# Sixteen-head cross-attention: rows of the stacks split by head parity, and the largest scores sought on four quarters of the array

## What is computed

```
q = rope(norm(x) @ cq.T)   split in 16 heads of 8 features
k = rope(ctx @ ck.T), v = ctx @ cv.T
scores = einsum('bqhd,bkhd->bhqk', q, k) / sqrt(8)
scores = where(mask, -inf, scores);  w = softmax(scores)
out    = einsum('bhqk,bkhd->bqhd', w, v)
```

## Time and profile before

| | us |
|---|---|
| median of 3 runs | 6767.78 |
| lowest and highest run | 6764.62, 6768.18 |
| the profiled execution | 6758.11 |
| its span | 6756.3 |

### The profile page before, as it was taken

The page is one execution under the profiler, slowest core; times in us unless marked ns, Lnnn a source line. Parts: engine busy times, 40 slices in busy tenths (PEclk is TensorE's granted clock), DMA queues, the critical chain, the costliest instruction groups (busy, mean ns, idle before and its releaser), DMA issues.

```text
span 6756.3 us, 141162 instructions
## 1 busy us (share of the span) xinstructions
PE 6176.6 (91%) x56181; PEld 4441.0 (66%) x56181; DVE 3931.5 (58%) x8705; ACT 3318.7 (49%) x6385; POOL 2240.2 (33%) x2179
## 2 busy tenths in 40 slices
PE   5799999999999999999979899999689999989998
PEld 4466666666666656666644777777457777766983
DVE  2677777777777777777755244444434444444553
ACT  1466656666566566665643234444223333333763
POOL 3555555555555555555520000000001111137440
PEclk6799999999999999999989799999789999998998
DMA  1566656656566566665730000000000000021000
GB/s 46 89 103 95 101 96 101 101 90 109 87 102 109 86 99 102 98 102 90 116 68 18 13 33 33 28 33 24 13 25 13 15 15 10 15 76 39 2 1 22
DMA packets 396487, 407.88 MB, mean 60 GB/s; under 512 B 125575, under 2 KB 372946, under 8 KB 393786
## 3 DMA queue, kind: packets, MB, share of 16 engines
q1 hardware_dynamic: 395834, 398.85, 33.3%
HBM read 158.00 MB, written 0.46 MB: 23 GB/s over the span
## 4 chain that ended last, share of the span: by engine, by line
PE 70%; DVE 9%; POOL 7%; issue 6%; ACT 4%; DMA 2%; SPq 1%; POOLq 1%; DVEq 0%; ACTq 0%
PE psum L2205 10%; PE psum L2172 9%; PE psum L1546 6%; PE psum L1534 6%; PE psum L1520 6%; PE psum L2217 4%; PE psum L1560 4%; PE psum L1568 3%; PE psum L1666 3%; POOL slot_context L3361 2%; DVE row_max L1885 2%; PE psum L435 2%; PE psum L421 2%; PE psum L1675 1%; DMA key_stack<-key_parts 1%
## 5 line engine op out<-in xcount | busy, mean ns | idle before, releaser
L1885 DVE TENSOR_REDUCE row_max<-psum 112x1 f32<-112x500 f32 x2304 | 1443.7, 669 | 282.8 <-PE psum L1534 277.7
L2003 ACT ACTIVATE weights<-psum 125x448 f32<-125x448 f32 x2304 | 1154.0, 544 | 764.0 <-PE psum L1520 749.7
L1520 PEld LDWEIGHTS psum<-query_stack,key_stack 121*125 121x125 bf16 x9216 | 829.0, 140 | 367.6 <-issue 165.7
L1534 PE MATMUL psum<-key_stack,query_stack 97*112 97x500 bf16 x2304 | 906.9, 394 | 102.8 <-DVE row_max L1885 81.9
L1520 PE MATMUL psum<-query_stack,key_stack 121*125 121x112 bf16 x9216 | 931.3, 224 | 70.1 <-ACT weights L2003 64.9
L2729 POOL TENSOR_TENSOR l_ctx_v<-l_ctx_v,l_ctx_w 125x512 f32<-125x512 f32 x48 | 60.9, 1269 | 2292.0 <-DVE l_ctx_v L2723 2292.0
L2205 PE MATMUL psum<-l_ctx_v,l_turned 125*128 125x128 f32 x5376 | 713.8, 281 | 16.0 <-ACT l_turned L2243 12.4
L2285 DVE TENSOR_REDUCE l_stat<-psum 128x1 f32<-128x1500 f32 (+1 forms) x224 | 391.7, 1748 | 573.4 <-PE psum L2172 573.4
L2205 PEld LDWEIGHTS psum<-l_ctx_v,l_turned 125*128 125x128 f32 x5376 | 643.3, 191 | 58.7 <-ACT l_turned L2243 40.0
L1546 PE MATMUL psum<-weights,values 125*17 125x112 f32 x18432 | 677.3, 265 | 0.2 <-ACT weights L2003 0.2
L1546 PEld LDWEIGHTS psum<-weights,values 125*17 125x17 f32 x18432 | 379.2, 97 | 263.1 <-ACT weights L2003 144.8
(11 more groups left out here) (526 smaller groups left out, 10283.8 us busy)
## 6 DMA issues: line engine op xcount, KB each, us to landing
key_stack<-key_parts SPq DMA_DIRECT2D x1728, 125.0 KB, 4.4
ctx_t<-in_ctxT SPq DMA_DIRECT2D x96, 750.0 KB
l_ctx_v<-in_ctxV SPq DMA_DIRECT2D x32, 750.0 KB
query_stack<-query_parts SPq DMA_DIRECT2D x576, 28.0 KB, 3.6
l_ctx_t<-in_ctxT SPq DMA_DIRECT2D x16, 750.0 KB
slot_context<-in_ctxV SPq DMA_DIRECT2D x16, 750.0 KB
key_stack<-ctx_mask_rows SPq DMA_DIRECT2D x576, 3.9 KB
sm_w<-in_sm_w SPq DMA_DIRECT2D x3, 2048.0 KB
```

Source lines behind the costliest of these rows:

```text
L1520: mm = e.matmul(self.k.psum[0:KN, h, (p % 4) * QC:(p % 4 + 1) * QC], ks[:, p, kt * KN:(kt + 1) * KN], q[:, p * QC:(p + 1) * QC])
L1534: e.matmul(self.k.psum[0:QC, 2 + n % 2, 0:500], q[0:ROWS_MAX, p * QC:(p + 1) * QC], ks[0:ROWS_MAX, p, c * 500:(c + 1) * 500]).then_inc(sel ...
L1885: e.tensor_reduce(self.largest[:, i % PAIRS, i // PAIRS:i // PAIRS + 1], k.psum[0:QC, 2 + i % 2, 0:500], AX.X, ALU.max, negate=True).then_ ...
L2003: e.activation(half(self.p[kt % 2], h), self.k.psum[0:KN, h, 0:HALF], ACT.Exp).then_inc(self.exped.sem, 1)
```

## The change

The stack of a pair now has 128 rows: 64 for each head of the pair. In each half, the six parts' 8 rows lie at rows 0, 8, 16, 24, 48 and 56, the mask at row 32, and 12 rows of maxima (three parts of one head's maxima for each two neighbouring pairs, four times) behind it; rows up to 47 are filled with zeros. Each DMA that wrote 16 rows becomes two that write 8. The largest scores of four heads (two pairs) are found by four matmuls of 64 rows by 64 columns, on the four quarters of the array, into two banks with 128 partitions; they are issued together, once a step, after the first score group, and wait until both banks of the step before are read. The extra rows of the query stack must be clear of the last use's maxima while the maxima are sought, which two new VectorE copies do for each slot (`clear_vector`, at kt = 7).

The core of the diff:

```diff
+PAIRS, F1 = H // 2, D // H
+PART_ROW = (0, 8, 16, 24, 48, 56)
...
-            self.k_stack = [sb(f"key_stack{i}", [ROWS_ALL, PAIRS, L], BF16) for i in range(3)]
-            self.q_stack = [sb(f"query_stack{i}", [ROWS_ALL, PAIRS * QC], BF16) for i in range(3)]
+            self.k_stack = [sb(f"key_stack{i}", [128, PAIRS, L], BF16) for i in range(3)]
+            self.q_stack = [sb(f"query_stack{i}", [128, QW + 8], BF16) for i in range(3)]
...
         for i, j in enumerate(K_PARTS):
-            e.dma_start(dst[F2 * i:F2 * i + F2, :, c * 500:(c + 1) * 500], part[:, j, :]).then_inc(sem, 16)
+            for h in range(2):
+                row = 64 * h + PART_ROW[i]
+                e.dma_start(dst[row:row + F1, :, c * 500:(c + 1) * 500], part[64 * h:64 * h + 64, j, :]).then_inc(sem, 16)
...
             for n in range(6):
-                e.dma_start(dst[ROWS:ROWS + 1, :, n * 250:(n + 1) * 250],
-                            self.mask_rows[6 * b + n:6 * b + n + 1, :].unsqueeze(1).broadcast_to(
-                                [1, PAIRS, 250])).then_inc(self.mask_stacked.sem, 16)
+                for row in (32, 96):
+                    e.dma_start(dst[row:row + 1, :, n * 250:(n + 1) * 250],
+                                self.mask_rows[6 * b + n:6 * b + n + 1, :].unsqueeze(1).broadcast_to(
+                                    [1, PAIRS, 250])).then_inc(self.mask_stacked.sem, 16)
...
         for i, part in enumerate(Q_PARTS):
-            e.dma_start(dst[F2 * i:F2 * i + F2, :].rearrange("j (p c) -> j p c", p=PAIRS),
-                        self.q_part[:, part, :]).then_inc(sem, 16)
+            for h in range(2):
+                row = 64 * h + PART_ROW[i]
+                e.dma_start(dst[row:row + F1, 0:QW].rearrange("j (p c) -> j p c", p=PAIRS),
+                            self.q_part[64 * h:64 * h + 64, part, :]).then_inc(sem, 16)
...
     def max_tensor(self, e, b, n):
...
+            e.wait_ge(self.cleared.sem, self.cleared(b))
...
-        if (b, n) > (0, 1):
-            e.wait_ge(self.max_read.sem, self.max_read(b, n) - 2)
-        e.matmul(self.k.psum[0:QC, 2 + n % 2, 0:500], q[0:ROWS_MAX, p * QC:(p + 1) * QC],
-                 ks[0:ROWS_MAX, p, c * 500:(c + 1) * 500]).then_inc(self.max_scored.sem, 1)
+        if (b, n) > (0, 0):
+            e.wait_ge(self.max_read.sem, self.max_read(b, n) - 1)
+        for h in range(2):
+            for j in range(2):
+                lo = (p + j) * QC + h * S
+                mm = e.matmul(self.k.psum[64 * j:64 * j + 64, 2 + h, 0:500], q[64 * h:64 * h + 64, lo:lo + 64],
+                              ks[64 * h:64 * h + 64, p + j, c * 500:(c + 1) * 500])
+            mm.then_inc(self.max_scored.sem, 1)
...
                     if 0 <= s < NS:
                         self.score_tensor(e, s, kt, h)
-                    if self.max_at(s, kt):
-                        b, n = self.max_at(s, kt)
-                        self.max_tensor(e, b, n + h)
+                    if h == 0 and self.max_at(s, kt):
+                        self.max_tensor(e, *self.max_at(s, kt))
...
+    def clear_vector(self, e, b):
+
+        if b >= 3:
+            e.wait_ge(self.scored.sem, self.scored(b - 3, KT - 1, 1))
+        for h in range(2):
+            op = e.tensor_copy(self.others(b, h, 16), self.no_max[64 * h + 32:64 * h + 48, :].unsqueeze(2).unsqueeze(
+                3).broadcast_to([16, TWOS, 2, S]))
+        op.then_inc(self.cleared.sem, 1)
...
-        e.tensor_copy(self.q_stack[b % 3][ROWS:ROWS_ALL, :].rearrange("r (p c) -> r p c", p=PAIRS),
-                      rows.unsqueeze(1).broadcast_to([1 + 3 * PAIRS, PAIRS, QC])).then_inc(self.side.emptied(*key), 1)
+        for h in range(2):
+            op = e.tensor_copy(self.others(b, h, OTHERS_USED), rows[32 * h:32 * h + OTHERS_USED, :, :].unsqueeze(
+                1).broadcast_to([OTHERS_USED, TWOS, 2, S]))
+        op.then_inc(self.side.emptied(*key), 1)
...
-                        e.tensor_reduce(self.largest[:, i % PAIRS, i // PAIRS:i // PAIRS + 1], k.psum[0:QC, 2 + i % 2, 0:500], AX.X,
+                        e.tensor_reduce(self.largest[:, TWOS * h + p // 2, c:c + 1], k.psum[:, 2 + h, 0:500], AX.X,
                                         ALU.max, negate=True).then_inc(self.max_read.sem, 1)
                 self.fixed_vector(e, s, kt)
+                if kt == 7 and 3 <= s + 2 < NS:
+                    self.clear_vector(e, s + 2)
```

## The result

The changed kernel takes 7636.52 us, the median of 4 runs (7628.34 to 7651.61), beside 6767.98 us for the kernel before (4 runs): a ratio of 1.1286 with a 95% interval of 1.1265 to 1.1307. It is slower by 868 us. The profiled execution took 7628.34 us, its span is 7626.5 us, against 6758.11 and 6756.3 before.

The account below looks back on a forecast made before the run. SyncE's DMA issues were taken to bound the changed kernel: 96 slots of 42.7 us make 4099, less 3241 now, +858 on 6758 gives 7616, about 7625 us with the median's 9.7. The range was 7260 to 8090.

Parts of the forecast that it names:

- Does half the size halve the issue? The rows say no.: SyncE's queue: a half-size copy holds it as long as a full one, taken as 0.705 us an issue.
- 42.7 us a slot: SyncE's time for 60 issues at 0.705 us plus 0.4 for the fetch, above the 34.3 that TensorE needs.
- the key chain at kt 10 and 11: Steps feeding the next slot's first key copy, partly at low clock: nothing to 2 us a slot, taken as nothing.
- The prologue, "2 us": Longer memsets of the prologue, together with the transpose of the maxima once a slot, were costed at 2 us.
- VectorE's work: Split rows copy and two clearing copies add 0.6 to 1.9 us a slot, taken as 0.8, hidden beside TensorE.
- I take the four as one: TensorE's four quarter matmuls run side by side and take 0.22 us a step together.
- The change of shape: TensorE: each change costs 0.08 us; two more a step make 184 us over 1152 steps.
- the gain of 58 us on TensorE: Quarters gain 242 us, less 184 for changes of shape, leaving 58, not reaching the sum because of SyncE.
- rival B: SyncE: half-size issues take half the time and stay hidden, so TensorE's gain shows: 6526 to 6710 us; chance 0.06.
- Rival A: Transfers bound too: copies to 8 partitions move at 63 GB/s, 47.5 us a slot, 8087 us; chance 0.27.
- The two directions of the waits: SyncE's waits are eaten up; TensorE waits once a slot, at kt = 10, for query DMAs, idling some 8 us.

Follow-up runs that it names:

- e1_tiny: The kernel before, with a copy of three rows of 32 bytes to scratch behind each of a slot's 30 stack copies, so 60 issues: 7633.51 us.
- e6_noclear: e2_rows16 without the two clearing copies of a slot: 6988.14 us.
- e4_own: e2_rows16, but each bank's two quarter matmuls wait only for the reduction of their own bank: 6993.94 us.
- e8_full: e4_own with two matmuls over the whole array in place of the four quarters: 6885.86 us.
- e2_rows16: The changed kernel with 30 issues a slot again, each part copied by one DMA of 16 rows, only row 32 getting the mask: 7011.64 us.
- e9_order: The kernel before with both full largest-score matmuls behind the second score group: 6806.88 us.
- e5_order: e4_own with the four quarter matmuls moved behind both score groups, next to the value products: 6900.57 us.

## Why the prediction was right

The forecast was 7625 us, the measured median is 7636.5, and the mechanism is the one forecast: e1_tiny has the issues and nothing else of the change, and takes 7633.5 us. That the number is within 12 us is partly luck, as errors of opposite sign met. Point by point:

- **"Does half the size halve the issue? The rows say no."** Right: 609 ns for 62.5 KB, 649 ns for three rows of 32 bytes (e1_tiny). The shape did matter a little, 567 against 623 ns for masks of four and of eight pairs, which was not foreseen.
- **42.7 us a slot.** From the first key copy to the last are 4320.6 - 211.8 = 4108.8 us, 42.8 a slot. The number came out so near because two parts offset each other: an issue took 0.68 us with its gap ((4108.8 - 152) / 96, less 0.4, over 60), not 0.705, and SyncE still waited 1.6 us a slot, which had been taken as nothing: about 1 us before the first key copy of most slots, the key chain at kt 10 and 11, and some 5 us in most second slots of a phase, which TensorE sets.
- **The prologue, "2 us".** Mis-sized: the first key copy comes 16.9 us later. The copies of ones start 15.5 us later, behind VectorE's first six clearing copies, and hold SyncE 703 ns each, not 640. The six take 16.2 us where later ones take 0.55 each, and nearly all of it is in two: one takes 2.9 us and ends at 55.9 us, the next takes 10.3 us and ends at 66.2 us. Two of GpSimd's memsets of the key stack, 10 us each, end at 55.7 and 65.9. So VectorE seems to have stood until GpSimd was done; no run tests it. The lines view of VectorE for 40 to 75 us has the six as its costliest group:

```profile
L1810 DVE COPY query_stack<-no_max 16x448 bf16<-16x448 bf16 x6 | 16.2, 2698 | 0.2
```

- **VectorE's work.** The two rows copies take 0.38 us each and the two clearing copies 0.55: 1.25 us a slot more, where 0.8 was taken. It is hidden under SyncE, as said; without SyncE's bound part of it shows (e6_noclear).
- **The quarters.** "I take the four as one" was right: 0.41 us for four. (The row it leant on was misread in part: the transposes it calls full-width have 56 columns of weights, and take 0.46 us, not 0.44.) The change of shape was mis-sized: 0.08 us was taken from one gap. Now each group's own 0.22 us is followed by 0.10, 0.11 and 0.14 us (1104.20, 1104.52, 1104.85, 1105.21), 0.35 together where the one gap of before was 0.08: 0.27 paid for 0.22 saved. So the gain of 58 us on TensorE is a loss of 0.05 x 1152 = 58 us, which e4_own against e8_full bears out (0.6 us a slot at full clock). The Trainium skill (TensorEngine Tiling (Array Packing), Tiling Modes) says that a change of mode drains TensorE; the trace agrees, with 0.10 to 0.14 us a boundary.
- **What lay under SyncE.** The prediction never priced the changed kernel without SyncE as the bound except in rival B, at 6526 to 6710 us. e2_rows16 took 7012 (with both banks' wait and all of VectorE's work). B would have been wrong even with free issues. What it lacked is shown in part: the quarters cost 58 us where they were to gain 58 to 242, the prologue costs some 20, and the clock, which B left out, is lower in some of the long slots (0.82 where it was 0.96, e9_order). The rest is argued: both engines run near their limit in the short slots (of a slot of 26.42 us before, TensorE is busy 25.77 and VectorE 21.15), and each was priced alone. How the 103 us left in e8_full behind the prologue divide between layout, copies and place isn't settled; e6_noclear puts some 23 of them down to the clearing copies. e9_order moved the matmuls to another place than e8_full's, so its 44 can't be taken off here.
- **Rival A.** Its mechanism is shown (74 GB/s against 127), its price is not: transfers stay behind the issues. The Trainium skill (SBUF — State Buffer, Door 1: The DMA port swizzle) says bandwidth depends on the ports that the partitions reach; the two rates agree with that, but no run was made to tell ports from the number of engines at work. What the views show is the share falling with the rate: 53% busy at 74 GB/s, full at 127.
- **The two directions of the waits.** TensorE's matmuls wait for the queries 78 times, 527 us in all, 5.5 us a slot and not 8: a part of the stretching is matmuls at the low clock instead.

## What to carry to other kernels

Count the DMA issues, not only their bytes: a copy from SBUF to SBUF holds its queue for some 0.6 us whether it moves 96 bytes or 125 KB, and a queue that issues 30 of them in 33.8 us was taken for 21.6, nearly two thirds, though the page doesn't call it busy. Before work is packed on parts of TensorE's array, put a price on each change of shape (0.10 to 0.14 us here): four quarters in place of two full matmuls of 500 columns saved 0.22 us and paid 0.27. When a bound has been found, price the kernel without it too, by a run that takes only that bound away. And compare slot by slot with the granted clock beside it: only so did a cost of 44 us turn out to be seven slots at a lower clock and not a cost of every step.

## What was not expected

- A small change of order or work lowered TensorE's clock in some slots and not in others of the same work. Moving the first of two matmuls behind the second score group took the second slot of a phase from 42.65 to 48.40 us in seven of eleven phases (0.96 to 0.82, e9_order), and e5_order had 46.95 or 42.93 us (0.85 or 0.96) in one execution. With quarters the granted clock over block 0 was 0.94 (e4_own), with full matmuls in the same place 0.97 (e8_full). What decides it isn't settled: e9_order took no work away.
- Copies of 8 rows move 74 GB/s where copies of 16 rows move 127, and a 16-row copy by itself reaches 240 to 285. A copy of one row of four pairs is issued 56 ns faster than one of eight.
